# Causal attention scores: bias and row maxima in one VectorE instruction per head, rounding in one pass, new lists of chains

## The chip, the cores and the metric

The kernel runs on one core of a Trainium2 chip: TensorE (PE) with its weight loads (PEld), VectorE (DVE), ScalarE (ACT), GpSimd (POOL) and the queue of SyncE (SP), each with a list of instructions of its own. The metric is the device time of one execution in microseconds. The kernel before took 3366.53 us as the median of three runs (3358.0 to 3366.66); the profiled execution is a fourth.

## The reference

A decoder of six pre-norm blocks, each added to x, over 64 sequences of 128 tokens of 256 numbers (16 heads of 16), in fp32:

```python
x = x + window_attention(layernorm(x))          # stage a: 7 keys around each token
x = x + masked_attention(layernorm(x), ctx)      # stage b: keys, values from ctx, mask by lengths
x = x + slot_memory(layernorm(x))                # stage f: routing to 64 slots, a GRU step
x = x + causal_attention(layernorm(x))           # stage 1: changed
x = x + cross_attention(layernorm(x), ctx)       # stage x
x = x + conv_mlp(layernorm(x))                   # stage g: changed at its end

def causal_attention(x):                         # per head, 128 x 128 scores
    att = q @ k.T * scale + bias                 # bias: learned from positions, -inf above the diagonal
    return (softmax(att, -1) @ v) @ Wproj + bproj

def conv_mlp(x):
    h = bit_linear(x, w1)                        # x rounded to 8 bits, w1 to -1, 0, 1
    h = silu(depthwise_conv1d(h, conv_w, conv_b))
    return bit_linear(h, w2)                     # h rounded: round(h * 127 / max|h|) per token
```

Softmax needs the maximum of every row of `q @ k.T + bias`, and the last `bit_linear` needs `h` rounded to whole numbers.

## The kernel before

The sequences are worked off by four chains of instructions, chain 0 to chain 3. A chain takes two sequences at a time through all six stages, 8 turns in all, and owns two of the eight PSUM banks, so that four pairs of sequences are under way at any moment. Each stage is a Python generator per engine (`maxima_vector`, `causal_scalar`, `causal_tensor`, `mlp_vector`, ...) that yields after each step; chains, engines and stages are tied by one counting semaphore for each chain and engine, and a wait names the event that it wants (`TABLES` numbers them).

What runs next on an engine is fixed beforehand: `ORDER` holds, for each engine, one digit per step, the chain that goes on. `in_order` reads the digits. An engine never skips an instruction that waits, so a chain that is late holds up the three others on that engine. Within a turn the chains are staggered: PE's list has chain 2 about 0.4 of a turn behind chain 3 in the kernel before.

The causal stage (events with the tag `1`) works on units u of 4 heads of 16 and one sequence, 8 units for a pair of sequences. For one unit PE writes scores of 4 heads to a bank (L1212); `maxima_vector` on DVE adds the bias (L692, 128x512, PSUM to SBUF), waits for itself, and takes the negative row maxima (L696, `negate=True`); ACT makes four exponentials of 128x128 with that maximum as bias (L1034); PE transposes them (L1284), ACT copies them to SBUF (L1041), PE multiplies with the values (L1221). The same `maxima_vector` serves stages b and x without a bias: there L696 reads PSUM, and nothing is added. `max_of` gives the column of `chain_m` that belongs to one head.

At the end of stage g, DVE multiplies the gated rows by their scale (L904, once for each of the two sequences), ACT adds the constant 12582912 (L1156), which drops the fraction, and DVE takes it off again and writes bf16 (L908); PE then multiplies with the second weight matrix (L1468), and DVE adds the result to x (L913).

In the names of rows, `banks` is PSUM, `chain_arena` the SBUF region in which most of a chain's buffers overlap, `chain_m` the row maxima, `pos_bias` the bias.

Of the kernel before, what the change touches and what calls it, by code (L numbers as in the profile page):

```python
# [11 lines left out]
ALU = mybir.AluOpType  # L12
# [10 lines left out]
B = 2  # L23
# [15 lines left out]
class Events:  # L39
# [10 lines left out]
    def now(self, name):  # L50
# [24 lines left out]
        f_y 1_st0 1_st1 1_mv0 1_mv1 1_ve 1_bi0 1_mx0 1_bi1 1_mx1 1_bi2 1_mx2 1_bi3 1_mx3 1_bi4 1_mx4 1_bi5 1_mx5  # L75
        1_bi6 1_mx6 1_bi7 1_mx7 1_rc 1_o 1_y x_st0 x_st1 x_mv0 x_mv1 x_ve x_mx0 x_mx1 x_mx2 x_mx3 x_mx4 x_mx5 x_mx6
        x_mx7 x_rc x_o x_y g_st0 g_st1 g_mv0 g_mv1 g_ve g_am g_cl g_rc g_bk g_sc g_q2 g_hp0 g_hp1 g_t00 g_t01 g_t20
        g_t21 g_si0 g_hp2 g_t02 g_t03 g_t22 g_t23 g_si1 g_hp3 g_t04 g_t05 g_t24 g_t25 g_si2 g_t06 g_t07 g_t26 g_t27
        g_si3 g_ax g_ah g_clh g_rch g_bkh g_sch g_mu0 g_mu1 g_r20 g_r21 y0 y1""".split(),
# [7 lines left out]
        g_c1 g_c2 g_c3 g_th0 g_c4 g_c5 g_th1 g_c6 g_c7 g_th2 g_th3 g_ro0 g_ro1""".split(),  # L87
# [13 lines left out]
        "0011223330310212303102123300112233001122330011223300112233001122"),  # L101
    "pool": (
        "3012330011223012333300301201112223001231201320132012303013320012331133220000333330300011130022120211"
        "1131212202312220123132033010012333321100033330332230010011001301222111311201222220213213203320100333"
        "1323113330030320322011000100310222311111102122220221321320332010033313231133300303203220110001003102"
        "2231111110212222022132132033201003331323113330030320322011000100310222311111102122220221321320332010"
        "0333132311333003032032201100010031022231111110212222022132132033201003331323113330030320322011000100"
        "31022231111110212222022132132033201001211222"),
    "vector": (
        "3012333333000300031110222131133221332023313030021300320112201012021331121023232103321332000000112200"  # L110
        "1111113222233220331030333113030330101002012203311001122331112200223232220011330030032211301221003333"
        "2332331100220010000112333332213310311333013301311220330223322003220300033100330300110301010211003330"
        "0122033112312011322121122123220003323003302323123031031300110012113300233203030133202022211100200111"
        "0011002223112121123131212131321302233223301103211232312120112003300220220223302200133110033121001221"
        "3111330210121220223302333312331202001111223003300100220031332332133311333203323331100211301102313100"
        "3320300030002200220022333122033101300100130311013313131331131300032000311310212033212331103312213310"
        "1002002201020222220022111300111002330021002212232311131213331311130331122200112221133112011020330200"
        "2222022223302020133112230022132231221001111010113333330033222110002211232222331200300321003320031331"
        "3333133232131032230303333020113211001101100022003330333000230321203313103303030303013132211022122111"
        "2211331000113310033013310112110112200002012000302220022323222111221121002001230023003223323223132331"  # L120
        "1111111101130302221122211331120110200300222022320222002233111322002231223122100111101011333333003322"
        "2110002211232222331200300321003320031331333313323213103223030333302011321100110110002200333033300023"
        "0321203313103303030303013132211022122111221133100011331003301331011211011220000201200030222002232322"
        "2111221020112001230023003223323223132331111111110113030222112221133112011020030022202232022200223311"
        "1322002231223122100111101011333333003322211000221123222233120030032100332003133133331332321310322303"
        "0333302011321100110110002200333033300023032120331310330303030301313221102212211122113310001133100330"
        "1331011211011220000201200030222002232322211122102011200123002300322332322313233111111111011303022211"
        "2221133112011020030022202232022200223311132200223122312210011110101133333300332221100022112322223312"
        "0030032100332003133133331332321310322303033330201132110011011000220033303330002303212033131033030303"
        "0301313221102212211122113310001133100330133101121101122000020120003022200223232221112210201120012300"  # L130
        "2300322332322313233111111111011303022211222113311201102003002220223202220022331113220022312231221001"
        "1110101133333300332221100022112322223312003003210033200313313333133232131032230303333020113211001101"
        "1000220033303330002303212033131033030303030131322110221221112211331000113310033013310112110112200002"
        "0120003022200223232221112210201120012300230032233232231323311111111101130302221122211331120110200300"
        "2220223202220022331113220022312231221001111010113333330033222110002211232222331200300321003320031331"
        "3333133232131032230303333022011110011021100200000020022000100110202122122112211111111111112111221122"
        "22222222222222222222"),
    "scalar": (
        "3012330301312302003131102230211220123330001211322333303030130011031013231210323103032013210210231300"
        "3321032321332130320133032300312100201023303113203200103033230030011031220100201011322301231231322122"  # L140
        "0120112022132003213112132232132031012031003131303023230323322303001031110010123100320120302213231123"
        "1013102310212231201221032120020322020013133121213010032113232131323212030202303030230311301330003303"
        "3132012230331031301331331230201323301321003120200201303231300301203210213032003021330120210011021011"
        "3012321301031121301223103201131221232122223310321103120330212203230103312132211202023000300120231021"
        "0221300130131331202130112132021130102101210102013033202221122132323321232132130100131323132001302030"
        "3230203203213211330300233320330112301330313101333132301203330132130013000100313021001203013203020012"
        "0122001012310302312031121310203023110121320123133311313122301201133101303221032022022101223223120110"
        "0320322020302301023103210221320112313122200122101113103103110102102122202203113230312323232132212012"
        "2012123032311323230302300102303203330132121203033302333203301102301101331330102330133232001310100100"
        "3130210012030132030200120122001012310302312031121310203023110121320123133311313122301201133101303221"  # L150
        "0320220221012232231201100320322020302301023103210221320112313122200122101113103103110102102122202203"
        "1132303123232321322120122012123032311323230302300102303203330132121203033302333203301102301101331330"
        "1023301332320013101001003130210012030132030200120122001012310302312031121310203023110121320123133311"
        "3131223012011331013032210320220221012232231201100320322020302301023103210221320112313122200122101113"
        "1031031101021021222022031132303123232321322120122012123032311323230302300102303203330132121203033302"
        "3332033011023011013313301023301332320013101001003130210012030132030200120122001012310302312031121310"
        "2030231101213201231333113131223012011331013032210320220221012232231201100320322020302301023103210221"
        "3201123131222001221011131031031101021021222022031132303123232321322120122012123032311323230302300102"
        "3032033301321212030333023332033011023011013313301023301332320013101001003130210012030132030200120122"
# [523 lines left out]
def maxima_vector(e, c, n, tag, k, bias=False):  # L683

    t, pe, dve, done = c.t, c.pe.of(n), c.dve.of(n), c.dve.now
    for u in range(B * GROUPS):
        b, r = u // GROUPS, row_group(u)
        e.wait_ge(*pe(f"{tag}_s{u}"))
        if bias:
            if u >= 4:  # L690
                e.wait_ge(*pe(f"{tag}_pT{u - 4}"))
            e.tensor_tensor(flat(t["s"][:, u % 4]), c.ps[:, u % 2, :], flat(k["pos_bias"][:, r]), ALU.add).then_inc(*done(f"{tag}_bi{u}"))  # L692
            e.wait_ge(*dve(f"{tag}_bi{u}"))
# [1110 lines left out]
```

## Time and profile before

| | us |
|---|---|
| median of 3 runs (lowest, highest) | 3366.53 (3358.0, 3366.66) |
| profiled execution, its own time | 3359.88 |
| its span, first to last instruction | 3358.1 |

Busy means that an instruction of the engine was running; the rest of the span is idle. A row of the windows lists for each engine the busy microseconds in that stretch, with the number of instructions in brackets, then PE's granted clock as a share of full speed, the share of the DMA engines and GB/s. A row of the timeline gives start, length, engine, line and operation; `x2` behind it merges two neighbours, and a bracket tells how long the engine sat idle before it and for whom. A turn is counted from one chain's store of its results to its next store; from 1641.50 us on a turn takes 395.5 to 396.2 us, and its pattern repeats until the last. Most rows below lie in the turn from 1641.50 to 2037.66 us, called the settled turn.

### The profile page before, as it was taken

The page shows a single profiled execution, that of the slowest core. Times are in us where ns is not written, and L with a number is a line of the kernel's source. Part 1 is how long each engine was busy: PE and PEld are TensorE (multiplying, and loading weights), DVE is VectorE, ACT ScalarE, POOL GpSimd, SP SyncE. Part 2 cuts the span into 40 slices and gives each one's busy share as a digit, 9 for nine tenths or more (in the row PEclk, how much of TensorE's full clock was granted, in tenths as well). Part 3 has the DMA queues.
Part 4 walks back from the last instruction along what each step waited for, and adds up shares of the span by engine and source line. Part 5 has one row for each costly group of instructions (what it writes and reads, how often), then busy time and mean ns, then how long its engine had stood idle before and what let it go on. Part 6 is the DMA issues. An engine that isn't in the chain of part 4 may idle for free.

```text
span 3358.1 us, 59674 instructions
## 1 busy us (share of the span) xinstructions
PE 2939.3 (88%) x23279; PEld 2077.8 (62%) x23406; DVE 2527.9 (75%) x5446; ACT 2180.8 (65%) x4271; POOL 753.5 (22%) x1360
## 2 busy tenths in 40 slices
PE   3799986999879998899988998899988998889984
PEld 3556754666656766567655666567665676556763
DVE  6846598756897579975897768976798758887676
ACT  2258763577646876577855777657765677557773
POOL 1420013300232112320133102321032301232000
PEclk8899997999999999999999999999999999999996
DMA  4000010000000000000000000000000000000000
GB/s 154 1 1 1 4 26 16 1 1 5 23 12 9 1 15 12 20 1 1 15 23 9 1 4 16 20 9 1 5 22 15 6 1 15 12 20 1 1 1 13
DMA packets 43467, 43.47 MB, mean 13 GB/s; under 512 B 8576, under 2 KB 41184, under 8 KB 43184
## 3 DMA queue, kind: packets, MB, share of 16 engines
q1 hardware_dynamic: 41200, 36.46, 3.7%
q8 instruction: 184, 3.01, 0.4%
q10 hardware_dynamic: 1984, 3.18, 0.3%
q14 instruction: 99, 0.81, 0.1%
HBM read 31.24 MB, written 8.39 MB: 12 GB/s over the span
## 4 chain that ended last, share of the span: by engine, by line
PE 59%; DVE 23%; ACT 9%; issue 4%; POOL 3%; DMA 1%; SPq 0%; DVEq 0%; POOLq 0%; ACTq 0%
PE banks L1179 9%; PE banks L1212 9%; PE banks L1258 6%; PE banks L1320 4%; PE banks L1221 4%; DVE chain_m L696 4%; PE banks L1197 3%; PE banks L1254 3%; PE banks L1284 3%; DVE chain_arena L890 2%; PE banks L1404 2%; PE banks L1299 2%; DVE chain_arena L774 2%; ACT chain_arena L1013 2%; PE banks L1344 2%
## 5 line engine op out<-in xcount | busy, mean ns | idle before, releaser
L1212 PE MATMUL banks<-chain_arena 64*128 64x256 f32 x3072 | 438.5, 407 | 39.3 <-DVE chain_m L696 28.2
L696 DVE TENSOR_REDUCE chain_m<-banks 128x4 f32<-128x512 f32 x512 | 329.3, 683 | 113.2 <-PE banks L1212 111.5
L1513 POOL TENSOR_SCALAR chain_ng<-chain_sv 128x2 f32<-128x2 f32 x192 | 52.9, 276 | 1448.5 <-DVE chain_sv L677 1448.4
L1212 PEld LDWEIGHTS banks<-chain_arena 64*128 64x128 f32 x3072 | 273.8, 189 | 168.0 <-issue 85.6
L1034 ACT ACTIVATE chain_arena<-chain_arena,chain_m 128x128 f32<-128x128 f32 x1024 | 323.8, 392 | 27.7 <-DVE chain_m L696 25.0
L968 ACT ACTIVATE chain_xn<-chain_xa,chain_nm,chain_rs 128x256 f32<-128x256 f32 x384 | 209.2, 595 | 163.3 <-POOL chain_nm L1517 162.6
L1258 PE MATMUL banks<-chain_arena 64*128 64x256 f32 x2048 | 295.1, 407 | 0.0
L1258 PEld LDWEIGHTS banks<-chain_arena 64*128 64x128 f32 x2048 | 178.7, 188 | 122.7 <-issue 110.6
L692 DVE TENSOR_TENSOR chain_arena<-banks,pos_bias 128x512 f32<-128x512 f32 x256 | 175.1, 684 | 105.4 <-PE banks L1212 105.3
L1221 PE MATMUL banks<-chain_arena,chain_va 128*32 128x128 f32 x5120 | 195.5, 279 | 35.4 <-ACT chain_arena L1013 23.0
L1013 ACT ACTIVATE chain_arena<-banks,chain_mask_k 128x1024 f32<-128x1024 f32 x128 | 142.4, 1113 | 103.3 <-PE banks L1258 102.5
L1567 POOL TENSOR_TENSOR chain_arena<-chain_arena 128x512 f32<-128x512 f32 x128 | 168.8, 1336 | 155.4 <-DVE chain_arena L774 155.2
L1179 PE MATMUL banks<-chain_arena,wqkv0T 128*128 128x256 f32 x768 | 188.7, 392 | 6.3 <-ACT chain_arena L975 6.3
L1013 ACT ACTIVATE chain_arena<-banks 128x1024 f32<-128x1024 f32 x128 | 131.6, 1028 | 95.0 <-PE banks L1258 94.3
L717 DVE TENSOR_TENSOR chain_xa<-banks,chain_xa 128x512 f32<-128x512 f32 x96 | 66.0, 688 | 165.2 <-PE banks L1320 165.1
L1221 PEld LDWEIGHTS banks<-chain_arena,chain_va 128*32 128x32 f32 x5120 | 126.7, 110 | 100.3 <-issue 37.8
L696 DVE TENSOR_REDUCE chain_m<-chain_arena 128x4 f32<-128x512 f32 x256 | 175.7, 686 | 8.8
L1284 PE MATMUL banks<-ident,chain_arena 128*128 128x128 f32 x1024 | 158.3, 281 | 14.2 <-ACT chain_arena L1034 13.6
L774 DVE TENSOR_TENSOR chain_arena<-banks,chain_arena 128x512 f32<-128x512 f32 x224 | 146.7, 683 | 28.8 <-PE banks L1369 19.6
L1254 PE MATMUL banks<-chain_xn,pick 128*128 128x512 bf16 x385 | 127.2, 385 | 45.5 <-ACT chain_arena L1013 20.9
L1179 PEld LDWEIGHTS banks<-chain_arena,wqkv0T 128*128 128x128 f32 x768 | 143.1, 194 | 34.4 <-ACT chain_arena L975 8.2
L1145 ACT ACTIVATE chain_arena<-chain_arena,pack 128x256 f32<-128x256 f32 x256 | 138.5, 595 | 32.6 <-DVE chain_arena L881 32.0
(314 smaller groups left out, 7013.2 us busy)
## 6 DMA issues: line engine op xcount, KB each, us to landing
chain_xn<-in_ctx SPq DMA_DIRECT2D x32, 256.0 KB, 2.8
chain_xa<-in_x SPq DMA_DIRECT2D x32, 256.0 KB, 3.1
out<-chain_xa SPq DMA_DIRECT2D x32, 256.0 KB, 2.2
chain_arena<-in_mask SPq DMA_DIRECT2D x32, 128.0 KB, 3.7
f_w1t<-in_w1t ACTq DMA_DIRECT2D x1, 1024.0 KB, 7.5
f_w2t<-in_w2t ACTq DMA_DIRECT2D x1, 1024.0 KB, 14.7
wqkv0T<-in_wqkv0T ACTq DMA_DIRECT2D x1, 768.0 KB, 17.1
whh<-in_whh SPq DMA_DIRECT2D x1, 768.0 KB, 10.3
```

The costliest lines, as they stand in the source:

```text
L692: e.tensor_tensor(flat(t["s"][:, u % 4]), c.ps[:, u % 2, :], flat(k["pos_bias"][:, r]), ALU.add).then_inc(*done(f"{tag}_bi{u}"))
L696: e.tensor_reduce(m, s.rearrange("p (j o) t -> p j o t", o=2), AX.X, ALU.max, negate=True).then_inc(*done(f"{tag}_mx{u}"))
L774: e.tensor_tensor(halves(ring[:, slot]), bank(c, w % 2), halves(t["vp"])[:, :, w:w + T], ALU.mult).then_inc(*done(f"a_pv{w}"))
L968: e.activation(t["xn"][:, b, :], t["xa"][:, b, :], ACT.Identity, scale=t["rs"][:, b:b + 1], bias=t["nm"][:, b:b + 1]).then_inc(*done(f"{ta ...
L1013: e.activation(flat(t["p"][:, u % 2]), flat(ps), ACT.Exp, bias=t["mask_k"][:, b:b + 1] if masked else 0.0).then_inc(*done(f"{tag}_ex{u}"))
L1034: ex = e.activation(s, s, ACT.Exp, bias=max_of(t["m"], u // GROUPS, row_group(u), a))
L1179: mm = e.matmul(c.ps[:, i, N * m:N * m + N], w[:, j, c0 + 128 * m:c0 + 128 * m + 128], flat(src[:, j]), start=(j == 0), stop=(j == KT - 1))
L1212: mm[i] = e.matmul(c.ps[:, i, 2 * T * j:2 * T * j + 2 * T], t["qh"][p, j, x, b, :], flat(t["kx"][p, j, b]), start=not masked, stop=not mas ...
L1221: mm = e.matmul(out[32 * a:32 * a + 32, :], c.t["va"][:, b, VH * h:VH * h + 32], p(a), start=True, stop=True)
L1254: e.matmul(ps[:, i, :], k["pick"][:, 2 * i + o, :], flat(t["mT"][:, b]), start=True, stop=False)
L1258: mm = e.matmul(ps[:, i, 2 * T * j:2 * T * j + 2 * T], t["kx"][p, j, b, o, :], t["qh"][p, j, :, b, :], start=False, stop=j == KT - 1)
L1284: mm = e.transpose(ps[:, u % 2, T * a:T * a + T], t["s"][:, u % 4, a, :], k["ident"][:])
```

## The change

Three things are changed.

1. In the causal stage the add and the reduction are replaced by `tensor_tensor_reduce`, one per head: it writes `(scores + bias) * -1` and, as its accumulator output, the least of these per row, which is the negative maximum. ACT's exponential takes the written scores with `scale=-1.0`. The events `1_bi0` to `1_bi7` are gone.
2. ACT's pass L1156 is gone; DVE's `tensor_scalar` adds and subtracts the constant in one instruction.
3. The five lists in `ORDER` are new for these steps: chains go first in the order 0, 2, 3, 1, where it was 3, 0, 1, 2.

```diff
@@ maxima_vector
-            e.tensor_tensor(flat(t["s"][:, u % 4]), c.ps[:, u % 2, :], flat(k["pos_bias"][:, r]), ALU.add).then_inc(*done(f"{tag}_bi{u}"))
-            e.wait_ge(*dve(f"{tag}_bi{u}"))
-        s = t["s"][:, u % 4] if bias else bank(c, u % 2)
+            for a in range(PER):
+                mx = e.tensor_tensor_reduce(t["s"][:, u % 4, a], bank(c, u % 2)[:, a], k["pos_bias"][:, r, a // 2, a % 2], -1.0, 3e38, ALU.add, ALU.min,
+                                            max_of(t["m"], b, r, a))
+            mx.then_inc(*done(f"{tag}_mx{u}"))
+            yield
+            continue
+        s = bank(c, u % 2)
@@ mlp_vector
-        e.wait_ge(*act(f"g_ro{b}"))
-        e.tensor_scalar(t["hq"][:, :, b, :], cv[:, :, b, :], -ROUND, None, ALU.add).then_inc(*done(f"g_r2{b}"))
+        e.wait_ge(*dve(f"g_mu{b}"))
+        e.tensor_scalar(t["hq"][:, :, b, :], cv[:, :, b, :], ROUND, -ROUND, ALU.add, ALU.add).then_inc(*done(f"g_r2{b}"))
@@ causal_scalar
-                ex = e.activation(s, s, ACT.Exp, bias=max_of(t["m"], u // GROUPS, row_group(u), a))
+                ex = e.activation(s, s, ACT.Exp, scale=-1.0, bias=max_of(t["m"], u // GROUPS, row_group(u), a))
@@ scalar_turn
-    for b in range(B):
-        v = t["cv"][:, :, b, :]
-        e.wait_ge(*dve(f"g_mu{b}"))
-        e.activation(v, v, ACT.Identity, bias=k["rounder"][:, 0:1]).then_inc(*done(f"g_ro{b}"))
-        yield
@@ ORDER, PE's list, first line
-        "3012330313023003130110202312333213313322000103001121220021321213122031323001023013230313013031302130"
+        "0231002030201220302332121010031031310020022222220333203313013312101120121032003201023201203213203021"
```

What it does to the instructions, first in the causal stage on DVE. Before, in the first turn, around the first unit of chain 3 (chain numbers are kept in the names):

```order
L851 TENSOR_TENSOR chain0_arena<-banks,bvo 128x256
L692 TENSOR_TENSOR chain3_arena<-banks,pos_bias 128x512
L696 TENSOR_REDUCE chain3_m<-chain3_arena 128x2x2
L692 TENSOR_TENSOR chain3_arena<-banks,pos_bias 128x512
L696 TENSOR_REDUCE chain3_m<-chain3_arena 128x2x2
L831 SCALAR_TENSOR_TENSOR chain1_arena<-banks,chain1_arena,gate_bias 128x512
L835 SCALAR_TENSOR_TENSOR chain1_arena<-banks,chain1_arena,new_bias 128x256
```

After, around the first unit of chain 0 (lines have moved: L831 is what was L827, L693 is new; ISA is the custom instruction):

```order
L830 RECIPROCAL chain3_arena<-chain3_arena 128x1
L831 COPY chain3_arena<-banks 128x128
L693 ISA chain0_arena,chain0_m<-banks,pos_bias 128x128
L693 ISA chain0_m 128x1
L693 ISA chain0_arena,chain0_m<-banks,pos_bias 128x128
L693 ISA chain0_m 128x1
L693 ISA chain0_arena,chain0_m<-banks,pos_bias 128x128
L693 ISA chain0_m 128x1
L693 ISA chain0_arena,chain0_m<-banks,pos_bias 128x128
L693 ISA chain0_m 128x1
L693 ISA chain0_arena,chain0_m<-banks,pos_bias 128x128
```

A unit was two instructions of 512 columns; it is now eight, four of 128 columns and four that write one accumulator column each, with no wait between them.

Second, DVE in a settled turn where one chain's gated rows are rounded while chain 3 works on its weighted values (L774, L778 after). Before:

```order
L904 TENSOR_TENSOR chain0_arena<-chain0_arena,banks 128x8x128
L774 TENSOR_TENSOR chain3_arena<-banks,chain3_arena 128x512 x2
L904 TENSOR_TENSOR chain0_arena<-chain0_arena,banks 128x8x128
L774 TENSOR_TENSOR chain3_arena<-banks,chain3_arena 128x512
L908 TENSOR_SCALAR chain0_arena<-chain0_arena 128x8x128
L774 TENSOR_TENSOR chain3_arena<-banks,chain3_arena 128x512
L908 TENSOR_SCALAR chain0_arena<-chain0_arena 128x8x128
L785 TENSOR_TENSOR chain3_arena<-chain3_arena 128x512
L913 SCALAR_TENSOR_TENSOR chain0_xa<-banks,chain0_qs,chain0_xa 128x256
L789 TENSOR_TENSOR chain3_arena<-chain3_arena 128x512
L913 SCALAR_TENSOR_TENSOR chain0_xa<-banks,chain0_qs,chain0_xa 128x256
```

After (L908 is what was L904, L912 what was L908, L917 what was L913):

```order
L908 TENSOR_TENSOR chain1_arena<-chain1_arena,banks 128x8x128
L843 SCALAR_TENSOR_TENSOR chain0_arena<-chain0_arena,half_hn 128x256
L845 TENSOR_TENSOR chain0_arena<-chain0_arena 128x256
L908 TENSOR_TENSOR chain1_arena<-chain1_arena,banks 128x8x128
L778 TENSOR_TENSOR chain3_arena<-banks,chain3_arena 128x512
L912 TENSOR_SCALAR chain1_arena<-chain1_arena 128x8x128
L778 TENSOR_TENSOR chain3_arena<-banks,chain3_arena 128x512 x2
L912 TENSOR_SCALAR chain1_arena<-chain1_arena 128x8x128
L917 SCALAR_TENSOR_TENSOR chain1_xa<-banks,chain1_qs,chain1_xa 128x256
L778 TENSOR_TENSOR chain3_arena<-banks,chain3_arena 128x512 x2
L917 SCALAR_TENSOR_TENSOR chain1_xa<-banks,chain1_qs,chain1_xa 128x256
```

The two multiplications of the gated rows now have two small instructions of another chain between them, and the rounding follows with one step of chain 3 in between, in the place in which it stood; the pass of ACT that it waited for is gone.

Third, the start of the chains on PE. Before:

```order
L1481 MATMUL banks<-ident,chain3_xn 128x128 x4
L1481 MATMUL banks<-ident,chain0_xn 128x128 x4
L1481 MATMUL banks<-ident,chain1_xn 128x128 x4
L1481 MATMUL banks<-ident,chain2_xn 128x128 x4
L1170 MATMUL banks<-ident,chain3_xn 128x128 x4
L1179 MATMUL banks<-chain3_arena,wqkv0T 128x256 x4
```

After:

```order
L1480 MATMUL banks<-ident,chain0_xn 128x128 x4
L1480 MATMUL banks<-ident,chain2_xn 128x128 x4
L1480 MATMUL banks<-ident,chain3_xn 128x128 x4
L1480 MATMUL banks<-ident,chain1_xn 128x128 x4
L1169 MATMUL banks<-ident,chain0_xn 128x128 x4
L1178 MATMUL banks<-chain0_arena,wqkv0T 128x256 x4
```

The names of the chains have changed places; the kinds of step stand as they stood, and the transposed contexts (L1481, L1480 after) of all four chains still come ahead of anything else. The tables of activation functions are loaded 69 times in either kernel.

## Rows read from the trace of the kernel before

**Rows 1.** The page: span, busy times by engine, last chain by engine.
```profile
span 3358.1 us, 59674 instructions
...
PE 2939.3 (88%) x23279; PEld 2077.8 (62%) x23406; DVE 2527.9 (75%) x5446; ACT 2180.8 (65%) x4271; POOL 753.5 (22%) x1360
...
PE 59%; DVE 23%; ACT 9%; issue 4%; POOL 3%; DMA 1%; SPq 0%; DVEq 0%; POOLq 0%; ACTq 0%
```

**Rows 2.** Windows: the second turn, a settled turn (columns as told above).
```profile
463.97:869.98 406.01, 348.29 (x2702) 242.25 (x2714) 299.65 (x646) 252.84 (x506) 89.71 (x164) 0.94 0.04 10
...
1641.50:2037.66 396.16, 360.12 (x2898) 255.49 (x2913) 308.40 (x668) 269.59 (x534) 93.84 (x168) 0.98 0.04 10
```

**Rows 3.** Windows: the settled turn cut in two.
```profile
1641.50:1880.00 238.50, 209.93 (x1623) 143.25 (x1631) 204.67 (x434) 144.81 (x265) 73.48 (x119) 0.96 0.05 15
1880.00:2037.66 157.66, 150.19 (x1276) 112.23 (x1282) 103.72 (x234) 124.78 (x269) 20.36 (x50) 1.00 0.01 3
```

**Rows 4.** Windows of L692 (causal add) alone, same two stretches.
```profile
1641.50:1880.00 238.50, 6.84 (x10) 0.96 0.05 15
1880.00:2037.66 157.66, 15.04 (x22) 1.00 0.01 3
```

**Rows 5.** Windows of L1156 (ScalarE's rounding) alone, same two stretches.
```profile
1641.50:1880.00 238.50, 6.68 (x6) 0.96 0.05 15
1880.00:2037.66 157.66, 2.29 (x2) 1.00 0.01 3
```

**Rows 6.** Waits of the settled turn: us in total, times, longest.
```profile
ACT chain_arena L1034 <- DVE chain_m L696: 2.0, 4, 0.9
```

**Rows 7.** Waits of PE over the whole run, same columns.
```profile
PE banks L1468 <- DVE chain_arena L908: 6.9, 9, 3.2
```

**Rows 8.** Groups on DVE by form: busy us, mean ns | idle before.
```profile
L908 DVE TENSOR_SCALAR chain_arena<-chain_arena 128x1024 bf16<-128x1024 f32 x64 | 48.1, 759 | 4.5 <-ACT chain_arena L1156 4.5
...
L478 DVE TENSOR_SCALAR f_w1t<-f_w1t 128x2048 f32<-128x2048 f32 x1 | 1.2, 1227 | 0.0
...
L480 DVE TENSOR_SCALAR w1t<-f_w1t 128x2048 bf16<-128x2048 f32 x1 | 1.2, 1226 | 0.0
```

**Rows 9.** Groups on ACT by form, same columns.
```profile
L1156 ACT ACTIVATE chain_arena<-chain_arena,rounder 128x1024 f32<-128x1024 f32 x64 | 72.4, 1149 | 42.1 <-DVE chain_arena L904 42.1
```

**Rows 10.** Timeline of DVE: two causal units; columns: start us, length us, instruction.
```profile
1882.75 0.69 DVE L692 TENSOR_TENSOR chain_arena<-banks,pos_bias 128x512 f32<-128x512 f32 x1 [0.60 <-PE banks L1212]
...
1884.08 0.68 DVE L692 TENSOR_TENSOR chain_arena<-banks,pos_bias 128x512 f32<-128x512 f32 x1
```

**Rows 11.** Timeline of DVE: instructions that wait for nothing in between.
```profile
1904.67 0.08 DVE L809 MATCH_VALUE_LOAD chain_arena<-chain_arena 128x8 f32 x1
1904.74 0.21 DVE L809 MATCH_REPLACE8 chain_arena<-chain_arena 128x64 f32<-128x64 f32 x1
1904.87 0.08 DVE L809 MATCH_VALUE_LOAD chain_arena<-chain_arena 128x8 f32 x1
...
1986.12 1.28 DVE L696 TENSOR_REDUCE chain_m<-banks 128x4 f32<-128x512 f32 x2
1987.31 0.68 DVE L863 TENSOR_REDUCE chain_qs<-chain_xn 128x2 f32<-128x512 f32 x1
```

**Rows 12.** Timeline of DVE: instructions that each wait for the last one.
```profile
1965.97 0.29 DVE L817 TENSOR_REDUCE chain_arena<-chain_arena 128x2 f32<-128x128 f32 x1
1966.30 0.17 DVE L819 RECIPROCAL chain_arena<-chain_arena 128x2 f32<-128x2 f32 x1
1966.49 0.29 DVE L821 TENSOR_TENSOR chain_arena<-chain_arena 128x128 f32<-128x128 f32 x1
```

**Rows 13.** Timeline: rounding of one chain's gated rows.
```profile
1694.85 2.19 ACT L1156 ACTIVATE chain_arena<-chain_arena,rounder 128x1024 f32<-128x1024 f32 x2
...
1696.04 0.69 DVE L908 TENSOR_SCALAR chain_arena<-chain_arena 128x1024 bf16<-128x1024 f32 x1 [0.20 <-ACT chain_arena L1156]
```

**Rows 14.** Timeline: PE's first instruction of a chain.
```profile
76.94 3.65 PE L1481 MATMUL banks<-ident,chain_xn 128*128 128x128 f32 x16 [15.45 <-DMA chain_xn<-in_ctx]
```

More of the change, by code:

```diff
@@ L74 @@
         f_top0 f_top1 f_sub f_mr0 f_mr1 f_m f_em f_s f_r f_al f_w1 f_w2 f_ac f_rz f_n1 f_n2 f_n3 f_u1 f_u2 f_u3 f_sv
[L75 to L79, printed above, removed]
+        f_y 1_st0 1_st1 1_mv0 1_mv1 1_ve 1_mx0 1_mx1 1_mx2 1_mx3 1_mx4 1_mx5 1_mx6 1_mx7 1_rc 1_o 1_y x_st0 x_st1
+        x_mv0 x_mv1 x_ve x_mx0 x_mx1 x_mx2 x_mx3 x_mx4 x_mx5 x_mx6 x_mx7 x_rc x_o x_y g_st0 g_st1 g_mv0 g_mv1 g_ve
+        g_am g_cl g_rc g_bk g_sc g_q2 g_hp0 g_hp1 g_t00 g_t01 g_t20 g_t21 g_si0 g_hp2 g_t02 g_t03 g_t22 g_t23 g_si1
+        g_hp3 g_t04 g_t05 g_t24 g_t25 g_si2 g_t06 g_t07 g_t26 g_t27 g_si3 g_ax g_ah g_clh g_rch g_bkh g_sch g_mu0
+        g_mu1 g_r20 g_r21 y0 y1""".split(),
     "setup_act": """
@@ L86 @@
         x_xn0 x_xn1 x_xnT x_q x_k x_v x_mT x_ex0 x_ex1 x_ou0 x_ex2 x_ex3 x_ou1 x_oc g_xn0 g_xn1 g_q1 g_bc g_xqT g_c0
[L87 removed]
+        g_c1 g_c2 g_c3 g_th0 g_c4 g_c5 g_th1 g_c6 g_c7 g_th2 g_th3""".split(),
     "setup_pe": """
@@ new lines @@
+        "0231002233110231000022220303232311101332113102301231020320032213310000222110000233030322220232333023"
+        "3111012131112113103102100232200300100033022120020113332222232032333303111231111213110130210021322003"
+        "0033122200002001022221123323032333311123031311112113010312001230002203100033022012020221122333223023"
+        "3330311321312111113101301200213220030033122200002001022221123323032333311123031311112113010312001230"
+        "0022031000330220120202211223332230233330311321312111113101301200213220030033122200002001022221123323"
@@ new lines @@
+        "03233331112303131111211301031200123223133111"),
+    "vector": (
+        "0231000000222022203332111033131100200302202022012230202331233230101130012231300322001313122122113333"
+        "1133330111121100220020203200021223030201122233300133131311100313223111002200223300022113323300002200"
+        "1133003223322112222011330033103303300200100200210200200322020112311310003102231102332232033323233200"
+        "0323020032221032201210030030333002220303222010123211100112133322030332200232002121132123331331122330"
+        "3223100223122111310100100033002001112211133110033211233211222001121112220011333001122111101130322303"
+        "3332233300220010011233002211331111133012211002233202220300011000330000011020003311020330023031123302"
+        "2222221222000221000212032023222110201100103200103110320033333322233322233003320013003313003313213222"
+        "2122222111212113330333221101012231312203302230313003303130131101301012133223300333311120011122112220"
+        "0211121321002113131011303223011333322111131313220000002200213322113301331022101221133202102200301001"
+        "0310030000200011330203300231103233021212222200022200022112203212232230212310300203330030303011332220"
+        "1101122121330023003200300222322122323312331212310113100122112211122133223033301013100131013133113312"
+        "3303130223030111111233213320012330022331112110011211221100302211331100112211332230030033003002233312"
+        "1133022101033101111331021212020023302002200030011003031010000020113322332332000112233000212220221212"
+        "2022300211030121031222003202031003113233333330222033020223003002132313232233212231221231102211011033"
+        "3123332112213022032200331331001330313131011301031212233003333223311100221112221120022111111111300113"
+        "3220001132231131131133223003030300220021331122330013301101012210033221220221000130010303000010100020"
+        "3322113302333320112222220002220002211220321223223021231030020333003030301133222011011221213300230032"
+        "0030022232212232331233121231011310012211221112213322303330101310013101313311331233031302230301111112"
+        "3321332001233002233111211001121122110030221133110011221133223003003300300223331211330221010331011113"
+        "3102121202002330200220003001100303101000002011332233233200011223300021222022121220223002110301210312"
+        "2200320203100311323333333022203302022300300213231323223321223122123110221101103331233321122130220322"
+        "0033133100133031313101130103121223300333322331110022111222112002211111111130011332200011322311311311"
+        "3322300303030022002133112233001330110101221003322122022100013001030300001010002033221133023333201122"
+        "2222000222000221122032122322302123103002033300303030113322201101122121330023003200300222322122323312"
+        "3312123101131001221122111221332230333010131001310131331133123303130223030111111233213320012330022331"
+        "1121100112112211003022113311001122113322300300330030022333121133022101033101111331021212020023302002"
+        "2000300110030310100000211332233321132332221222221212222232112322112312131133333333333333133333113311"
+        "11111111111111111111"),
```

146 lines of the change are left out of this document (56 added, 90 removed).

## The prediction

> **What bounds the kernel now.** I read the page's busy times first, then the chain that ended last, then windows by turn, and only then the lines of the change. PE is busy 2939.3 of 3358.1 us, DVE 2527.9, ACT 2180.8, and the chain runs 59% through PE, 23% through DVE and 9% through ACT [rows 1]. No work of PE is removed, so all that can be won lies in PE's 419 idle microseconds. A settled turn takes 396.16 us, in which PE is idle for 36.0 [rows 2]. Cut in two, the turn has two limits [rows 3]. In its first 238.5 us DVE is busy 204.7 (86%) and PE idle 28.6: DVE and PE share the limit there. In its last 157.7 us PE is busy 150.2 (95%) and DVE idle 54.0: there PE alone is the limit. What the change does to DVE is worth something in the first part and next to nothing in the second. The causal stage lies mostly in the second: of 32 adds (L692) in the turn, 10 stand in the first part and 22 in the other [rows 4]; of 8 rounding passes on ACT, 6 stand in the first [rows 5].
>
> **The change part by part.** Durations are those of the profiled execution, which took 3359.88 us; the median of the three runs is 6.6 us higher, and the runs fall on both sides, so I make the sum against 3360 and add 3 for the median.
>
> *Causal units on DVE.* A unit now takes 1884.08 − 1882.75 = 1.33 us, from one add to the next with the reduction and its wait between them [rows 10]. The trace has no `tensor_tensor_reduce` and no accumulator read, so I bound them. What counts is not the length of an instruction but the step from its start to the next start. Where nothing is waited for, lengths overlap: two reductions of 512 columns take 1987.31 − 1986.12 = 1.19 us, 0.595 each, though each is listed with 0.68; a MATCH_REPLACE8 of 64 columns is followed after 0.13 us and a MATCH_VALUE_LOAD of 8 columns after 0.07 [rows 11]. A line through 64 and 512 columns has 1.04 ns for a column and 0.066 us fixed; for 128 columns it gives 0.20 us. A read of one column is nearest to the load, 0.07: it too is the small half of a pair that shares state inside the engine. The unit is then 4 × (0.20 + 0.07) = 1.08 us, 0.25 less. The lower bound, a read that costs nothing, is 0.80, 0.53 less. The upper bound is the step that the trace shows where each instruction waits for the one before it: 0.33 us for 128 columns, 0.19 for a tiny one [rows 12]; the unit is then 4 × 0.52 = 2.08, 0.75 more. I take 1.08, since neither half carries a wait. On 256 units that is 64 us of DVE, but only the 10 in 32 of the first part can shorten the turn: 10 × 0.25 = 2.5 us a turn, 20 us in 8 turns. DVE is not the only limit there, so I take half: **−10 us**. For the other 22, PE's work hides the saving, and if the upper bound held, DVE's 54 idle us would hide most of 22 × 0.75 = 16.5. ACT waits for the causal maxima for 2.0 us a turn in all [rows 6], so an earlier maximum by itself wins little. ACT's `scale=-1.0` is a constant in an instruction that stays: 0.
>
> The Trainium skill, "VectorE: DVE Perf Modes", section "The DRAIN you can't avoid", speaks against the edit: after every DVE instruction the pipeline is emptied before the next starts, and it advises fewer instructions. By that rule eight instructions for two would put the unit near the upper bound. The trace does not agree where nothing is waited for: the starts in [rows 11] are 0.08 us closer than the lengths allow. It does not show the custom pair, though, in which the read needs the last column of the one before.
>
> *The rounding.* ACT loses 64 passes of 1149 ns, 72.4 us of busy time [rows 9], 9 us a turn, on an engine that is idle in a third of it. DVE's pass keeps its size; a second constant operation costs nothing, since over 2048 columns two take 1227 ns and one 1226 [rows 8]. The step that goes is the way over ACT: from the start of ACT's pass to that of DVE's 1696.04 − 1694.85 = 1.19 us [rows 13], at most twice in each of 32 chain turns, 76 us, if all of it were on the path. But PE waited for L908 only 6.9 us in the whole run [rows 7], and that is my value: **−7 us**. DVE's own wait for ACT, 4.5 us [rows 8], is inside it. What is late next is the multiplication L904 ahead, with PE's two small products before it. One hazard: without ACT between them, DVE's two heavy passes follow each other and hold another chain's step by 0.6 us; the lists put one step of chain 3 between the two roundings, as before.
>
> *The lists.* Every engine's list is new, and here only bounds are to be had. At the start nothing is won: PE's first chain instruction waited 15.45 us for a context [rows 14], and in the new list the transposes of all four contexts still stand first, so the last load decides as before. At best the lists spread DVE's work so evenly that PE's idle share in the first part, 12%, falls half the way to the 5% of the second: 28.6 becomes 20, 8.6 us a turn, **−65** over the seven and a half full turns. At worst the turns settle like the second one of before, 406.01 us against 396.16 [rows 2]: 10 us a turn, **+80**. Between them I go by the freed time: 8 us of DVE and 9 of ACT a turn leave the first part with some 5 us less of DVE and 7 less of ACT, and I let 2 us of that reach the turn: **−16 us**.
>
> Sum: 3360 − 10 − 7 − 16 = 3327; with 3 for the median, 3330 us.
>
> **The rivals.**
>
> *A: the pair is slow.* The accumulator read waits until the 128 columns are through, and the next head waits for the read. The place is the causal unit on DVE, the price up to 0.75 us a unit; DVE's instruction list is in order, so the other chains' steps behind it are late too. In the first part 10 × 0.75 = 7.5 us a turn, 60 in all; in the second, hidden but for about 1 us a turn, 8. Less 7 for the rounding and with lists built for a cheaper unit: 3360 + 60 + 8 − 7 = 3421, 3424 as a median. It decides from a pair of 0.33 us on, where four of them make the 1.33 of before; at 0.40 it costs 0.27 a unit and gives about 3378. For it: the read depends on the last column. Against it: MATCH_VALUE_LOAD and MATCH_REPLACE8 depend on each other in the same way and start 0.07 us apart.
>
> *B: hidden anyway.* DVE's saving falls where PE is busy 95%, ACT was never the limit, and the new lists are one more arrangement of the same kind. Then only the 7 us of the rounding and a few by the lists, either way, are left: 3352 to 3372, 3358 in the middle. For it: the 2.0 us in [rows 6] and the place of the 22 units.
>
> *C: the lists win much.* The chains meet so that DVE is less full in the first part: 3360 − 65 − 17 = 3278, 3281 as a median. For it: 28.6 of a turn's 36.0 idle us lie in one part. Against it: the total of DVE, 300 of 396 us, remains, and the same first part must hold the window stage and the gated rows of four chains.
>
> **How the numbers follow.** A measurement of this kernel can tell about 0.3% from no change: 3356 to 3377. The forecast (3308 to 3350) has 0.42, A 0.25 (a third of it part of the way, at 3370 to 3400), B 0.20, C 0.13. Faster: 0.42 + 0.13 + 0.07 of B = 0.62. Same: 0.12 of B and 0.03 of A = 0.15. Slower: 0.22 of A and 0.01 of B = 0.23. The range leaves out half of C's far side and the upper half of A: 3278 to 3410. The likeliest case's own range is 3308 to 3350.
>
> **What would show each step.** The groups on DVE: the custom instruction with about 0.29 us listed and the next start 0.20 later, the read with 0.07 to 0.16; the timeline: the first starts of two units in a row 1.08 us apart (over 1.33 is A). DVE's busy sum near 2465 us. No line of ACT between L904 and L908 of before, and ACT's busy sum near 2108. Windows: a settled turn (over two turns, if they alternate) of 391 to 393 us with PE's idle near 32. Settled turns of 396 with a smaller DVE sum are B; below 388 are C; and a longer turn while the unit takes 1.08 us would mean that the lists, and not the pair, went wrong, which none of my cases prices at more than 80 us.

## The result and the profile after

| | before | after |
|---|---|---|
| median of five runs each (lowest, highest), us | 3366.02 (3356.91, 3366.66) | 3382.26 (3370.8, 3385.02) |
| ratio, 95% interval | | 1.0053 (1.0035 to 1.0071) |
| profiled execution, us | 3359.88 | 3370.8 |

The change makes the kernel 0.5% slower. The profiled execution of after is the quickest of its five. The page answers to [rows 1]:

```profile
span 3369.0 us, 61273 instructions
...
PE 2956.1 (88%) x23406; PEld 2077.0 (62%) x23406; DVE 2417.5 (72%) x6982; ACT 2112.4 (63%) x4207; POOL 731.7 (22%) x1360
...
PE 61%; DVE 21%; ACT 9%; issue 3%; DMA 3%; POOL 3%; SPq 0%; DVEq 0%; POOLq 0%; ACTq 0%
```

DVE is busy 110 us less, ACT 68 us less, and the time is longer. One trap lies in PE's row. After has 23406 matmul records, before has 23279 [rows 1]. The missing 127 are all of one line, as the group rows of PE show (line, tiles, count, busy us and mean ns, then the idle time before them), before first, after second:

```profile
L1254 PE MATMUL banks<-chain_xn,pick 128*128 128x512 bf16 x385 | 127.2, 385 | 45.5 <-ACT chain_arena L1013 20.9 <-ACT chain_arena L1017 8.7 <-ACT chain_xn L1004 8.1
```
```profile
L1253 PE MATMUL banks<-chain_xn,pick 128*128 128x512 bf16 x512 | 155.9, 387 | 58.4 <-ACT chain_arena L1017 35.4 <-ACT chain_xn L1008 15.0 <-ACT chain_arena L1021 7.1
```

So a part of what I read as idle time of PE in the kernel before was work that left no record. How much is seen beside a kernel with the same order and all 512 records, the one with the rounding alone changed (among the experiments below):

```profile
L1249 PE MATMUL banks<-chain_xn,pick 128*128 128x512 bf16 x512 | 155.6, 386 | 32.0 <-ACT chain_arena L1013 20.3 <-ACT chain_arena L1017 6.3 <-ACT chain_xn L1004 4.8
```

Its busy time for this line is 28 us longer, but only 45.5 − 32.0 = 13.5 us of that stood as idle time in before; the rest lies under the records of neighbouring matmuls, which overlap. The whole idle time agrees: 3361.5 − 2955.8 = 406 us there, 419 in before. I take 13 us for the missing records: PE's idle time in before was near 406 us, after has 413.

The two changed pieces came out as cheap as forecast, or cheaper. Groups on DVE, answering to [rows 8]:

```profile
L693 DVE CUSTOM_DVE_ANT_0 chain_arena<-banks,pos_bias 128x128 f32<-128x128 f32 x1024 | 226.2, 286 | 113.3 <-PE banks L1211 113.1
...
L693 DVE DVE_READ_ACCUMULATOR2_ANT chain_m<- 128x1 f32 x1024 | 84.8, 83 | 0.0
...
L912 DVE TENSOR_SCALAR chain_arena<-chain_arena 128x1024 bf16<-128x1024 f32 x64 | 46.0, 744 | 0.0
```

The timeline of DVE shows the step from head to head, answering to [rows 10]:

```profile
1643.47 0.28 DVE L693 CUSTOM_DVE_ANT_0 chain_arena<-banks,pos_bias 128x128 f32<-128x128 f32 x1
1643.67 0.08 DVE L693 DVE_READ_ACCUMULATOR2_ANT chain_m<- 128x1 f32 x1
1643.67 0.29 DVE L693 CUSTOM_DVE_ANT_0 chain_arena<-banks,pos_bias 128x128 f32<-128x128 f32 x1
...
1645.15 0.08 DVE L693 DVE_READ_ACCUMULATOR2_ANT chain_m<- 128x1 f32 x1
1645.15 0.69 DVE L885 TENSOR_TENSOR chain_arena<-banks,chain_arena 128x512 f32<-128x512 f32 x1
```

The read and the next head's instruction are recorded with the same start. Eight heads take 1645.15 − 1643.47 = 1.68 us, 0.21 each, so a unit of four takes 0.84 us against the 1.33 of before; 256 units × 0.49 = 125 us.

Where the time went is seen in windows. To have the same code on both sides I set after beside the first experiment below, which has the changed code and the lists of before. Each is cut at stores of its first chain: start-up and early turns, four whole turns, the rest (columns as in [rows 2]). After:

```profile
84.00:1231.23 1147.23, 1031.77 (x8135) 725.60 (x8133) 798.13 (x2368) 724.60 (x1454) 255.28 (x460) 0.96 0.03 8
1231.23:2842.26 1611.03, 1452.92 (x11648) 1019.35 (x11650) 1185.93 (x3440) 1046.34 (x2100) 363.37 (x672) 0.98 0.04 10
2842.26:3369.00 526.74, 438.13 (x3497) 304.53 (x3493) 380.88 (x1054) 318.35 (x634) 96.15 (x187) 0.94 0.03 10
```

Changed code, lists of before:

```profile
84.00:1248.15 1164.15, 1036.41 (x8133) 721.93 (x8132) 800.40 (x2363) 725.88 (x1461) 262.44 (x463) 0.95 0.03 8
1248.15:2822.02 1573.87, 1436.43 (x11650) 1018.76 (x11649) 1188.83 (x3441) 1042.98 (x2097) 371.67 (x672) 0.98 0.04 11
2822.02:3346.90 524.88, 441.73 (x3499) 308.98 (x3497) 385.18 (x1058) 317.36 (x630) 98.93 (x187) 0.94 0.03 10
```

The new lists are 16.9 us ahead after the early turns and lose 37.2 us in the four turns that follow: 402.8 us a turn against 393.5, with the same work (11,650 and 11,649 weight loads). Of the 37.2, 16.5 is PE's busy time and 20.7 its idle time. Their turns also alternate. Windows of two in a row:

```profile
1622.54:2035.66 413.12, 373.31 (x2963) 262.40 (x2963) 302.68 (x873) 263.18 (x527) 92.85 (x172) 0.97 0.03 10
2035.66:2428.33 392.67, 354.05 (x2867) 247.90 (x2864) 290.22 (x848) 259.40 (x522) 88.58 (x164) 0.98 0.04 11
```

The waits that have grown, over the whole run (us in total, times, longest), after first:

```profile
DVE chain_sums L709 <- PE banks L1298: 154.0, 51, 11.0
...
ACT chain_arena L1038 <- DVE chain_m L693: 63.9, 56, 4.5
...
DVE chain_stat L674 <- DMA chain_xa<-in_x: 35.6, 18, 6.2
PE banks L1253 <- ACT chain_arena L1017: 35.4, 38, 3.5
...
PE banks L1467 <- DVE chain_arena L912: 14.9, 13, 3.1
```

The same in the changed code with the lists of before:

```profile
DVE chain_sums L709 <- PE banks L1298: 75.7, 51, 4.6
...
PE banks L1253 <- ACT chain_arena L1017: 19.8, 25, 1.3
...
DVE chain_stat L674 <- DMA chain_xa<-in_x: 16.7, 6, 11.8
...
ACT chain_arena L1038 <- DVE chain_m L693: 10.8, 18, 1.7
...
PE banks L1467 <- DVE chain_arena L912: 5.7, 8, 3.0
```

ACT waits for the causal maxima (L1038) six times as long although the pair that makes them is the same instruction. That is the order, not the length. Not every wait grew, though. DVE's wait for the product that ends each of the masked, causal and cross-attention stages (L721) fell by more than L709's rose, after first:

```profile
DVE chain_xa L721 <- PE banks L1319: 83.6, 51, 5.7
```
```profile
DVE chain_xa L721 <- PE banks L1319: 186.5, 68, 8.0
```

### The profile page after: what moved, and what is told of

It reads as the page before. It is cut to its first block, busy times and chain, and to the rows that moved or that the text cites. A ratio compares the mean times of both kernels' runs of the same rounds, so it can differ in the third digit from the quotient of the medians.

```text
span 3369.0 us, 61273 instructions
## 1 busy us (share of the span) xinstructions
PE 2956.1 (88%) x23406; PEld 2077.0 (62%) x23406; DVE 2417.5 (72%) x6982; ACT 2112.4 (63%) x4207; POOL 731.7 (22%) x1360
## 4 chain that ended last, share of the span: by engine, by line
PE 61%; DVE 21%; ACT 9%; issue 3%; DMA 3%; POOL 3%; SPq 0%; DVEq 0%; POOLq 0%; ACTq 0%
PE banks L1178 10%; PE banks L1211 9%; PE banks L1257 7%; PE banks L1319 5%; PE banks L1220 4%; PE banks L1253 3%; PE banks L1196 3%; DVE chain_m L700 3%; PE banks L1283 2%; DVE chain_arena L693 2%; PE banks L1298 2%; ACT chain_arena L1017 2%; PE banks L1403 2%; PE banks L1169 2%; DVE chain_arena L778 1%
## 5 line engine op out<-in xcount | busy, mean ns | idle before, releaser
L1038 ACT ACTIVATE chain_arena<-chain_arena,chain_m 128x128 f32<-128x128 f32 x1024 | 320.6, 392 | 65.1 <-DVE chain_m L693 63.9
L693 DVE CUSTOM_DVE_ANT_0 chain_arena<-banks,pos_bias 128x128 f32<-128x128 f32 x1024 | 226.2, 286 | 113.3 <-PE banks L1211 113.1
L1253 PE MATMUL banks<-chain_xn,pick 128*128 128x512 bf16 x512 | 155.9, 387 | 58.4 <-ACT chain_arena L1017 35.4
L674 DVE BATCH_NORM_STATS2 chain_stat<-chain_xa 128x6 f32<-128x256 f32 x384 | 143.7, 416 | 40.1 <-DMA chain_xa<-in_x 35.6
L734 DVE TENSOR_TENSOR chain_arena<-chain_arena 128x512 f32<-128x512 f32 x192 | 125.8, 705 | 47.6 <-ACT chain_arena L1065 27.7
L778 DVE TENSOR_TENSOR chain_arena<-banks,chain_arena 128x512 f32<-128x512 f32 x224 | 145.8, 683 | 18.1 <-PE banks L1368 14.8
```

The costliest lines, as they stand in the source:

```text
L693: mx = e.tensor_tensor_reduce(t["s"][:, u % 4, a], bank(c, u % 2)[:, a], k["pos_bias"][:, r, a // 2, a % 2], -1.0, 3e38, ALU.add, ALU.min, ...
L778: e.tensor_tensor(halves(ring[:, slot]), bank(c, w % 2), halves(t["vp"])[:, :, w:w + T], ALU.mult).then_inc(*done(f"a_pv{w}"))
L1038: ex = e.activation(s, s, ACT.Exp, scale=-1.0, bias=max_of(t["m"], u // GROUPS, row_group(u), a))
L1253: e.matmul(ps[:, i, :], k["pick"][:, 2 * i + o, :], flat(t["mT"][:, b]), start=True, stop=False)
```

## The experiments

All ratios are to the kernel before on the same chip. A step is what one digit of `ORDER` releases. "Searched" lists were made by a program that adds up instruction lengths taken from the traces of before and after along queues and semaphores, moves steps, and keeps what makes the sum shorter; only the chip's times are given.

**Which part costs: the code in the old lists.**

```diff
 # e1_new_code_old_lists: the changed kernel
-ORDER = {"sync": ("0011223302302311... 
+ORDER = {"sync": ("0011223330310212...     # before's five lists, ScalarE's without its g_ro steps
 # e3_pair_only: the kernel before, its lists
-            e.tensor_tensor(flat(t["s"][:, u % 4]), ...)
+            for a in range(PER): mx = e.tensor_tensor_reduce(...)
 # e4_rounding_only: the kernel before, its lists without g_ro
-        e.tensor_scalar(..., -ROUND, None, ALU.add)
+        e.tensor_scalar(..., ROUND, -ROUND, ALU.add, ALU.add)
```

(The diffs are cut to their main lines. The events and ACT's `scale=-1.0` go with the pair, ACT's pass L1156 with the old rounding, here and below.)

> The changed code (pair per head, one-pass rounding) in the order of before; of ScalarE's list only the 64 rounding steps are gone. Theory L (the new lists cost the time): the two code terms of the forecast stand, 3366 - 10 - 7 = 3349, anything from 3345 to 3360. Theory I (the new instructions cost the time, in a way the DVE rows do not show): near the changed kernel, 3375 to 3385. A settled turn of one length, 393 to 396 us by L; 398 or more by I.

> Before with only the custom pair in the causal unit, old lists. Forecast's term: 10 us less, 3356. Since the unit takes 0.84 us and not the 1.08 assumed, up to twice that if DVE's time in the first part of a turn limits it: 3346. Theory I with the pair as the cause: 3375 or more. Hidden: 3364 to 3368. DVE busy about 110 us less than before in every case.

> Before with only the rounding in one DVE pass, old lists, ScalarE's rounding steps gone. Forecast's term: 7 us less, 3359. Hidden: 3364 to 3368. Theory I with the rounding as the cause (DVE's two passes in a row hold up other chains): 3372 or more. ACT busy about 72 us less than before in every case.

Measured: both parts 0.9971 (0.9957 to 0.9984), 3348.92 us; the pair alone 0.9961 (0.9948 to 0.9975), 3346.97 us; the rounding alone 1.0008 (0.9994 to 1.0022), 3360.3 us. The new instructions cost no time. In the old lists the pair is worth 13 us, the rounding nothing that can be measured, though ACT's busy time fell from 2180.8 to 2115.1 us. Theory I is out; the settled turn is 393.5 us, as theory L had it; of its terms the pair's stands and the rounding's does not. The same code in the new lists measured 1.0053, so changing the lists alone costs 1.0053 / 0.9971 = 1.0082 (1.0060 to 1.0105, from both intervals), 27 us.

**The other corner: the old code in the new lists.**

```diff
 # e2_old_code_new_lists: the kernel before
-ORDER = {"sync": ("0011223330310212...
+ORDER = {"sync": ("0011223302302311...     # after's lists, 64 g_ro steps put into ScalarE's
```

> The code of before in the new lists; ScalarE's 64 rounding steps are put back into its list at the first place after the multiplication they wait for. Theory L in its plain form (the two parts add up): the lists alone cost the 16 us measured plus the 17 of the code, 3399. Theory LF (lists are fitted to the lengths of the code they were made for, so both orders punish the other code): well above that, 3420 to 3450. Theory I: the lists are neutral, 3361 to 3371.

Measured: 1.0364 (1.0343 to 1.0386), 3480.49 us. This is 122 us over before and outside every plain sum: in the new lists the two parts are worth 1.0364 / 1.0053 = 1.0309, 105 us, where they are worth 10 in the old. Theory LF holds in its direction, and by more than its range; only half of it came, though: the new lists punish the old code, while the old lists do not punish the new code, which is 10 us faster in them. To see which part the new lists lean on, each was undone alone in them:

```diff
 # e10_new_lists_unit_undone: the changed kernel
-            for a in range(PER): mx = e.tensor_tensor_reduce(...)
+            e.tensor_tensor(flat(t["s"][:, u % 4]), ...); e.wait_ge(*dve(f"{tag}_bi{u}"))
 # e11_new_lists_rounding_undone: the changed kernel, g_ro steps put into ScalarE's list
-        e.tensor_scalar(..., ROUND, -ROUND, ALU.add, ALU.add)
+        e.tensor_scalar(..., -ROUND, None, ALU.add)
```

> The changed kernel with the causal unit of before (add, wait, reduction), its lists and the one-pass rounding kept. With both parts undone the new lists cost 3480. Theory U (it is the 0.49 us per unit, 125 us of DVE, that the new lists had spent): 3440 to 3470. Theory R (it is the way over ScalarE for the rounding): 3385 to 3400.

> The changed kernel with the rounding of before (ScalarE's pass, then VectorE's), its lists and the custom pair kept; the 64 rounding steps stand in ScalarE's list at the first place after the multiplication. Theory U: 3390 to 3405. Theory R: 3440 to 3475. The two undone parts together should give about the 3480 of both.

Measured: unit undone 1.0297 (1.0274 to 1.0321), 3459.77 us; rounding undone 1.0129 (1.0115 to 1.0144), 3403.25 us. Against after's 1.0053 that is 82 us for the unit and 26 for the rounding, together 108, beside the 105 of both. Theory U holds. So the new lists need the short unit: in them each of the 256 × 0.49 us counts for two thirds (82 of 125), in the old lists for a tenth (13 of 125). That DVE has less slack around the units in the new lists would explain it, but no run shows it. A part of the 82 us goes with TensorE's clock, which was granted at 0.959 with the unit undone and at 0.964 in after.

**Is the loss in one list?** From the changed kernel, one list altered by small shifts:

```diff
 # e7_pe_list_moved: TensorE's list, 1055 of 2944 steps at another place, 0.5 places on average
 # e8_dve_list_moved: VectorE's list, 1031 of 2720 steps, 0.6 places on average
```

> The changed kernel with TensorE's list alone altered: 1055 of its 2944 steps stand at another place, 0.5 places away on average and 10 at most. Theory P (the new lists lose where PE stands before a step whose input is late while another chain's step is ready): 20 to 45 us less than the changed kernel, 3337 to 3362. Theory D (DVE's list holds the loss, its steps that wait for PE's gate the others): within 10 us of the changed kernel.

> The changed kernel with VectorE's list alone altered: 1031 of its 2720 steps stand elsewhere, 0.6 places on average. Theory D: 20 to 40 us less than the changed kernel, 3342 to 3362, and L709's wait for L1298 (154 us in the changed kernel) near the 76 of the old lists. Theory P: within 10 us of the changed kernel. If both this and the kernel with TensorE's list altered gain, the loss is not in one list but in how the two fit.

Measured: TensorE's list 1.0033 (1.0020 to 1.0045), 3373.19 us; VectorE's 1.0004 (0.9989 to 1.0018), 3365.27 us. Against 1.0053 these are 7 and 16 us, and the first is not distinct from nothing. Theory P's 20 to 45 us did not come with this list; another alteration of it could still give them. VectorE's list gives some, but less than theory D's 20 to 40 and not by D's way: L709's wait for PE stayed at 155.3 us, so that wait, the one that grew most on DVE, need not go for the time to fall. Neither list alone, moved this little, gives back the 27 us. The lists of ScalarE, GpSimd and SyncE were not altered alone.

**Is it the gross order or many small misfits?** The two sets of lists differ by far more than the names of the chains. With the names exchanged so that they match best (old 0, 1, 2, 3 as new 2, 3, 1, 0), a step of TensorE's list stands 6.3 places from where it stood in the old list, on average, and up to 33. Below, single steps of four lists (all but SyncE's) are shifted by much less, from either set of lists, with the changed code:

```diff
 # e6_old_lists_searched: from before's lists, 0.6 to 0.9 places on average, at most 21
 # e12_new_lists_shifted: from after's lists, 0.5 to 0.9 places on average, at most 41
```

> The changed code in the lists of before, after the same shifting of single steps in four lists (without new priority rules). Theory L: 3349 (the changed code in the old lists) less 60 to 110 us, 3240 to 3290, and slower than the lists that were searched from the start. Theory H: 3340 or more.

> The changed kernel in its own lists, single steps of four lists shifted in the same way and as far as in the kernel that started from the old lists (0.5 to 0.9 places on average), which measured 0.9735 of before. Theory S (what costs is many small misfits of order, which both sets of lists hold, so both come to the same place when these are mended): ratio 0.969 to 0.979, 3256 to 3290 us. Theory G (the new lists lose by their gross order, the two-turn beat): at least 15 us more than the other kernel, 3290 or over.

Measured: from the old lists 0.9735 (0.9719 to 0.9751), 3273.93 us; from the new 0.9773 (0.9755 to 0.9790), 3283.93 us. Shifts of less than one place on average take 79 us (0.9971 − 0.9735, on 3360) from the old lists and 94 us (1.0053 − 0.9773) from the new. The 27 us between the two sets shrink to 13. Theory S holds in its range; G misses its 15 us narrowly, by less than the noise of the two ratios, and part of the loss may well be gross order, since the new lists stay behind. Their two-turn beat is still there (stores of one chain 383.3, 394.5, 384.8 and 400.4 us apart).

**Lists made from the start, for each code.**

```diff
 # e5_searched_lists: the changed kernel, five lists made anew
 # e9_old_code_searched: the kernel before, five lists made anew for it, same search
```

> The changed code, all five lists made anew by a search that starts from many priority rules and then shifts single steps. Theory L (the loss lies in the order alone, and PE's idle time is to be had by order): the 413 idle us of PE in the changed kernel fall by a third to a half, 3382 - 140 to 3382 - 200 = 3180 to 3240. Theory H (the chip punishes any list that is packed more tightly, as it did the old code in the new lists): 3340 or more.

> The code of before in lists that the same search made for it. Question: is the change of instructions worth anything once each code stands in lists of its own? Theory C (the DVE time that the pair saves is usable): the changed code in its searched lists measured 3210; the old one needs 125 us more of DVE (256 units by 0.49), of which a third to a half reaches the time: 3250 to 3275. Theory N (the lists are all, the instructions nothing): 3205 to 3225.

Measured: changed code 0.9548 (0.9535 to 0.9562), 3209.9 us, which beats both kernels; old code 0.9723 (0.9710 to 0.9736), 3268.08 us. Both times lie in the ranges of theory L and theory C. With lists of its own for each, the change of instructions is worth 58 us, 1.8%. The search is not exhaustive for either, so the 58 us hold for these two sets of lists. The page of the changed code in searched lists:

```profile
span 3207.7 us, 61144 instructions
...
PE 2893.0 (90%) x23277; PEld 2051.7 (64%) x23406; DVE 2417.0 (75%) x6982; ACT 2100.7 (65%) x4207; POOL 733.0 (23%) x1360
...
PE 50%; DVE 26%; ACT 13%; issue 5%; POOL 3%; DMA 3%; SPq 0%; DVEq 0%; ACTq 0%; POOLq 0%
```

DVE and ACT are as busy as in after. This trace lacks 129 records of L1253 again, for which I take the same 13 us; PE's idle time is therefore near 3207.7 − 2893.0 − 13 = 302 us, from 413. That is 111 of the 161 us between the two spans, a little over a quarter of the idle time and not the third to a half that theory L had counted on. The other 50 us are less busy time for the same matmuls, and with it goes the clock. The mean granted clock of TensorE, after first and the searched lists second:

```profile
core 0: 3369.0 us, clock 0.964
```
```profile
core 0: 3207.7 us, clock 0.982
```

## Why the prediction was wrong

*The bound.* Reading PE's idle time as all that can be won was right; its size was over-read by the 13 us or so of missing records, which the counts of [rows 1] give away: 23279 matmuls beside 23406 weight loads.

*The causal unit.* The mechanism was right: lengths overlap and the step between starts counts. The term was mis-sized. The read costs nothing beside the next head's instruction, so the unit takes the 0.84 us near my lower bound (0.80) and not 1.08. With that size, the rule that a third of the units (10 of 32) can shorten the turn and half of that reaches it gives 0.49 × 10 × 0.5 × 8 = 20 us; the pair alone measured 13 (8 to 17). The saving was taken too small and the share that reaches the turn too large, so that −10 came near is in part luck.

*The page against the edit.* The Trainium skill, "VectorE: DVE Perf Modes", section "The DRAIN you can't avoid", as I read it, would have put the unit near 2.08 us. The timeline above disagrees with that reading for this pair: the next head starts while the read is still listed. The section itself makes an exception, which my prediction left out: a next instruction that is not held starts earlier. It points to the same page's section "Two Vector instructions with no wait between them", which counts an accumulator output as two instructions. With the exception the trace agrees, at 0.21 us a pair beside 0.286 + 0.083 listed.

*The rounding, −7.* Measured −2 to +7 us in the old lists. The 6.9 us of [rows 7] were a real wait, but it only fell to 5.7 us in the changed code with the old lists, and in after it is 14.9. Here a smaller step failed: to take the whole wait for a pass as gone with the detour before it. Most of it stays; that the multiplication ahead (L904) is late as well would explain it, and is not shown.

*The lists, −16.* This is the step that failed, and it makes 43 of the 52 us between the forecast 3330 and the measured 3382. I let the time freed on DVE and ACT reach the turn by way of the new lists. Measured: +27 us (20 to 35). The bounds, −65 and +80, hold it, but the value was taken from the freed time, and freed time says nothing of what an order does: two orders for the same code lie 27 us apart, and small shifts of either move it by 79 and 94. The upper bound's reasoning, a turn like the second one of before (406 us), was nearer: 402.8. The last sentence of the prediction, a longer turn with a cheap unit, is what came; of the 0.23 that I gave to a slower kernel, 0.22 stood on a slow pair, and nearly nothing on the lists.

*The rivals.* A is refuted in its mechanism (0.21 us a head, where it decides at 0.33), though its sign came true. B's turn of 396 did not come; its remark that the new lists are one more arrangement of the same kind was the right one, and its "either way" should have been as wide as the lists' own bounds. C was to be had, but not by these lists: the searched ones went past its 3281.

What stays open: which steps of the new lists cost the 27 us. Neither PE's nor DVE's list alone gave them back, the other three were not tried alone, L709's wait is not needed for it, and the early turns even gain 17 us.

## What to carry to other kernels

An edit that shortens instructions and an order that is made anew are two changes, and the second can be the larger: run the new code in the old order, and the old code in the new, before judging either. The worth of a saved microsecond on an engine depends on the order it stands in, here 0.1 us in one set of lists and 0.66 in another. Where an engine's list is fixed beforehand and PE is idle for a tenth of the time, the order itself is worth working on first: here, with the changed code, it gave 142 us over the old lists (0.9971 to 0.9548), the edit in the old lists 10.

## What the runs showed of the hardware

**A custom reduction and its accumulator read.** 128 columns with a reduction take 286 ns as listed and the read 83, but a pair costs 0.21 us from start to start, with the read beside the next instruction. Eight such instructions (0.84 us) beat an add and a reduction of 512 columns with a wait between them (1.33 us).

**TensorE's clock moves the time beside the waits.** TensorE is granted one of two levels, 2.4 or 1.2 GHz, so a mean of c (as a share of 2.4 GHz) over a span means 2 × (1 − c) of the span at the lower. By the profiled executions that is 255 us in before (0.962), 243 in after (0.964), 248 in the changed code with old lists (0.963), 320 in the old code with new lists (0.954), and 115 in the searched lists (0.982). The kernel whose TensorE list was shifted had in its profiled execution about as much idle time as before (3374.5 − 2954.3 − 13 for the missing records = 407 us, beside 406), but 283 us at the lower level (0.958), and took 3376.31 us where before took 3359.88. The same shows between runs of one kernel. The five of after, clock and time: 0.964, 3370.8; 0.963, 3379.65; 0.962, 3382.26; 0.960, 3384.35; 0.959, 3385.02. A ranking by idle time alone would put the shifted list beside before and ahead of after (413 us, 3370.8). What decides the level in a stretch was not tried.
